# Taking the query projection from a transposed copy of x, with the layer norm folded into the weights and the rotation tables

## What is computed

```
xn   = layernorm(x)                       # per row: (x - mean) * (var + 1e-5)^-0.5
q    = rope(xn @ Wq);  k = rope(ctx @ Wk);  v = ctx @ Wv      # 32 heads of 16; ctx has 256 features
x1   = x + tanh(g_x) * (softmax(q k^T / 4) v @ Wout + bout)
r    = layernorm(x1)
y    = relu(r @ up)^2 @ down + (r @ expert) * (sum of the top 2 of r @ gate)
out  = x1 + tanh(g_f) * (layernorm(y) * gamma + beta)
```

## Time and profile before

| | |
|---|---|
| median of three runs | 1609.11 us |
| the profiled execution, its own time | 1609.51 us |
| its span in the trace | 1607.7 us (1.8 us lie around it) |
| PE busy | 1552.5 us, 97% |
| DVE busy | 976.1 us, 61% |
| ACT busy | 638.1 us, 40% |
| POOL busy | 296.2 us, 18% |
| DMA queue of the kernel | 27.8% of the 16 engines' span |

### The profile page before, as it was taken

How to read it: one execution, slowest core, us unless ns; L and a number is a source line. 1 busy time by engine, 2 the same in 40 slices (tenths; PEclk the granted TensorE clock), 3 DMA queues, 4 the chain that set the end, 5 groups by cost and what they waited for, 6 DMA issues and landing times.

```text
span 1607.7 us, 26049 instructions
## 1 busy us (share of the span) xinstructions
PE 1552.5 (97%) x9818; PEld 1158.5 (72%) x9818; DVE 976.1 (61%) x1448; ACT 638.1 (40%) x962; POOL 296.2 (18%) x370
## 2 busy tenths in 40 slices
PE   8799999999999999988999999999999999999997
PEld 6466666666666666654887887878878878788786
DVE  7887777887887777765663535426444354353524
ACT  4365555555555555556442222222222222222221
POOL 5222222222222222201010102002010020010202
PEclk9799999999999999999999999999999999999999
DMA  6644443444444344333530101101000011010101
GB/s 173 142 114 109 108 102 104 126 104 124 127 124 116 97 107 102 96 89 117 154 105 1 53 27 33 47 2 53 27 27 33 21 47 33 14 46 21 53 0 40
DMA packets 67192, 121.24 MB, mean 75 GB/s; under 512 B 12280, under 2 KB 25720, under 8 KB 67064
## 3 DMA queue, kind: packets, MB, share of 16 engines
q1 hardware_dynamic: 67064, 119.50, 27.8%
HBM read 51.17 MB, written 16.78 MB: 42 GB/s over the span
## 4 chain that ended last, share of the span: by engine, by line
PE 84%; DVE 11%; issue 2%; ACT 1%; POOL 1%; DMA 0%; POOLq 0%; DVEq 0%; ACTq 0%; SPq 0%
PE pP L986 16%; PE pA L1183 11%; PE pO L986 11%; PE pB L1183 11%; PE pT L986 10%; PE pO L1108 6%; PE pA L1080 6%; DVE mneg L1402 5%; PE pM L986 4%; PE pB L1096 2%; PE pT L993 2%; PE pP L993 2%; PE pM L993 2%; PE pM L1150 1%; DVE rot L1330 1%
## 5 line engine op out<-in xcount | busy, mean ns | idle before, releaser
L1402 DVE TENSOR_REDUCE mneg<-pA 128x4 f32<-128x1024 f32 x250 | 305.6, 1223 | 137.1 <-PE pA L1080 135.3
L887 ACT ACTIVATE probs<-pB 128x1024 f32<-128x1024 f32 x249 | 255.2, 1025 | 259.5 <-PE pB L1096 249.4
L1505 DVE TENSOR_TENSOR relu<-relu 128x512 f32<-128x512 f32 x128 | 89.0, 695 | 257.4 <-ACT hid L939 257.4
L704 POOL TENSOR_SCALAR var_eps<-meanvar 128x1 f32<-128x1 f32 x96 | 34.5, 360 | 1048.4 <-DVE meanvar L1287 1048.2
L1183 PE MATMUL pA<-dn,hid 128*128 128x512 f32 x768 | 198.6, 394 | 0.7
L1183 PE MATMUL pB<-dn,hid 128*128 128x512 f32 x768 | 196.0, 390 | 0.0
L986 PE MATMUL pP<-fT,up 128*128 128x512 f32 x768 | 190.3, 396 | 0.0
L986 PE MATMUL pO<-fT,up 128*128 128x512 f32 x768 | 187.6, 393 | 0.0
L1183 PEld LDWEIGHTS pA<-dn,hid 128*128 128x128 f32 x768 | 143.2, 188 | 35.7 <-DVE hid L1507 4.2
L986 PEld LDWEIGHTS pO<-fT,up 128*128 128x128 f32 x768 | 144.3, 188 | 32.6 <-issue 0.7
L1183 PEld LDWEIGHTS pB<-dn,hid 128*128 128x128 f32 x768 | 144.2, 188 | 31.0
(11 more groups left out here) (199 smaller groups left out, 1971.3 us busy)
## 6 DMA issues: line engine op xcount, KB each, us to landing
stk<-kT SPq DMA_DIRECT2D x180, 128.0 KB, 2.9
stq<-qT SPq DMA_DIRECT2D x180, 128.0 KB, 3.0
fres<-x_scratch SPq DMA_DIRECT2D x34, 256.0 KB, 2.8
xin<-x SPq DMA_DIRECT2D x32, 256.0 KB, 3.0
xres<-x SPq DMA_DIRECT2D x32, 256.0 KB, 3.3
x_scratch<-xres SPq DMA_DIRECT2D x32, 256.0 KB, 2.3
out<-y_s SPq DMA_DIRECT2D x32, 256.0 KB, 2.0
fx<-x_scratch SPq DMA_DIRECT2D x29, 256.0 KB, 2.7
```

The costliest lines, as they stand in the source:

```text
L704: nc.gpsimd.tensor_scalar_add(var_eps[:], meanvar[:, 1:2], EPS).then_inc(ve_made, 1)
L887: nc.scalar.activation(probs[:, s % 4, :, :, :].rearrange("p a b s -> p a (b s)"), psum[:, :, :], ACT.Exp).then_inc(exp_done, 1)
L1402: nc.vector.tensor_reduce(mneg[par][:, :, 2 * u:2 * u + 2].rearrange("p t q -> p q t"), psum[:, :, :].rearrange("p q (t k) -> p q t k", t= ...
L1505: nc.vector.tensor_tensor(r[:], r[:], r[:], ALU.mult).then_inc(sq_made, 1)
```

## The change

The query projection no longer starts from a normalised x that TensorE turns. The host gives a second copy of x, already turned, `xT`, with 128 features of each of four chunks on the partitions. With the weights Wq centred once (from each column its mean over the 512 features is subtracted), `x @ Wc` equals `(x - mean(x)) @ Wq`, so the mean of each row falls out. The row's `rstd` is a factor of each output row, and it is multiplied into this row tile's entries of the cosine and sine tables, after K has used them and before Q does.

What this does to the engines, for batches 2 to 15 (0 and 1 keep the old way in the opening):

- TensorE: X0 and X1 go (8 transposes an iteration). ScalarE: their two rounding copies go. VectorE: their two subtractions go, and the two `ln_apply`. The statistics stay.
- SP: `load_xT` twice an iteration, 256 KB each, into the tile `xn`; half 1 ahead of `load_x(i+3, 0)` and so of the residual, half 0 ahead of `load_x(i+3, 1)`. It waits until the half before has been split. `load_x` now waits for the statistics instead of `xn`.
- GpSimd: `split_x` twice an iteration (a rounding copy and a subtraction, 128x512 each): half 1 between `rope_sum` Q0 and `rope_sum` K1, half 0 after `rope_sum` Q1. TensorE's Q job waits for it (`xT_split`).
- VectorE: before each Q it scales two pieces of 128x32, of `cos_t` and of `sin_t`, and waits for both before the rotation.
- Once, at the end of the opening: 8 matmuls for the column means into pO, a copy of them by ScalarE (which takes part of its list ahead of the tanh of the gates), four transfers of Wq again, and on GpSimd 12 instructions of 128x512 (`centre_weights`). The first exponential and the fourth wait for 2 and 4 of the 4 chunks, since the raw weights lie in `probs`; Q0 of batch 2 waits for all.
- SBUF: `rden`, `aT`, `gt_s` and `gt_raw` move, two temporary tiles lie under `aT`, and there are two `rstd`.

```diff
@@ -65,12 +65,12 @@
...
-    0: ("X0", "a10"),
+    0: ("a10",),
...
-    5: ("X1", "kT0"),
+    5: ("kT0",),
@@ -217,6 +218,11 @@
...
             return first.enter_context(nc.sbuf_tensor(name, shape, dt))
+        def under(name, shape, dt=F32):
+            with nc.sbuf_tensor(name, shape, dt) as tile:
+                return tile
@@ -246,14 +252,19 @@
...
         attn = [sb1(f"attn{t}", [P, D]) for t in range(TT)]
-        rden = [sb1(f"rden{i}", [P, NH // 2]) for i in range(2)]
-        aT = [sb1(f"aT{i}", [P, KC, P], F32R) for i in range(2)]
+        aT = []
+        mean_w = under("mean_w", [P, P], F32R)
+        aT.append(sb1("aT0", [P, KC, P], F32R))
+        col_mean = under("col_mean", [P, D])
+        aT.append(sb1("aT1", [P, KC, P], F32R))
         xres = [sb1(f"xres{i}", [P, D]) for i in range(2)]
         gbout = sb1("gbout", [P, D])
+        rden = [sb1(f"rden{i}", [P, NH // 2]) for i in range(2)]
         mneg = [sb1(f"mneg{i}", [P, TT, NH]) for i in range(2)]
...
         rot2.append(sb1("rot21", [P, D]))
+        col_mean = col_mean[:, :]
         rot = {"Q0": rot_q0, "Q1": rot_q1, "K0": rot_k, "K1": rot_k}
@@ -261,6 +272,11 @@
...
         rot_k1 = raw1[0]
+        raw_again = [raw1[k] for k in (0, 1, 6, 7)]
+        def split_no(b, t):
+            return TT * (b - 2) + t + 1
@@ -493,9 +517,17 @@
...
                 if some(n - 1):
-                    sp.wait_ge(xn_made, n - 1)
+                    sp.wait_ge(xn_made if n <= TT * 2 + 1 else st_made, n - 1)
                 alone(sp)
                 sp.dma_start(xin[t][:], xt_d[n]).then_inc(x_in[t], INC)
+            def load_xT(b, t):
+                if (b, t) == (2, 0):
+                    sp.wait_ge(*done_of("X1", 1))
+                else:
+                    sp.wait_ge(xT_split, 2 * (split_no(b, t) - 1))
+                alone(sp)
+                sp.dma_start(xn[:], xT[b * TT + t]).then_inc(xT_in, INC)
@@ -549,6 +581,8 @@
...
+                if within(b2):
+                    load_xT(b2, 1)
@@ -558,6 +592,7 @@
...
+                    load_xT(i + 3, 0)
@@ -690,25 +730,49 @@
...
             last.then_inc(consts_made, 1)
+            nc.gpsimd.memset(mean_w[:].bitcast(F32), 1.0 / D).then_inc(mean_w_made, 1)
...
-            def inv_std(count):
+            def inv_std(count, t=0):
                 pool.wait_ge(mv_made, count)
...
                 pool.wait_ge(ve_made, count)
-                nc.gpsimd.tensor_tensor(rstd[:], var_eps[:], neg_half[:], ALU.pow).then_inc(rstd_made, 1)
+                nc.gpsimd.tensor_tensor(rstds[t][:], var_eps[:], neg_half[:], ALU.pow).then_inc(rstd_made, 1)
...
                 nc.gpsimd.tensor_tensor(t1, t1, rot2[ROPES.index(name) % 2][:], ALU.add).then_inc(roped, 1)
+            def split_x(b, t):
+                n = split_no(b, t)
+                used, of = ("Q0", b) if t else ("Q1", b - 1)
+                pool.wait_ge(*done_of(used, of))
+                pool.wait_ge(xT_in, INC * n)
+                alone(pool)
+                xv = xn[:].rearrange("p (c s) -> p c s", c=KC)
+                nc.gpsimd.tensor_copy(xnT[0][:], xv).then_inc(xT_split, 1)
+                pool.wait_ge(xT_split, 2 * n - 1)
+                nc.gpsimd.tensor_tensor(xnT[1][:], xv, xnT[0][:].bitcast(F32), ALU.subtract).then_inc(xT_split, 1)
+            def centre_weights():
+                pool.wait_ge(col_made, 1)
+                for c in range(KC):
+                    pool.wait_ge(w_again[c], INC)
+                    nc.gpsimd.tensor_tensor(raw_again[c], raw_again[c], col_mean, ALU.subtract).then_inc(centred, 1)
+                    pool.wait_ge(centred, 3 * c + 1)
+                    nc.gpsimd.tensor_copy(wq_s[0][:, c, :], raw_again[c]).then_inc(centred, 1)
+                    pool.wait_ge(centred, 3 * c + 2)
+                    nc.gpsimd.tensor_tensor(wq_s[1][:, c, :], raw_again[c], wq_s[0][:, c, :].bitcast(F32),
+                                            ALU.subtract).then_inc(centred, 1)
@@ -736,9 +800,17 @@
...
+                        if name == "Q0":
+                            split_x(b2, 1)
...
+                    if i < 0:
+                        split_ctx(i + 3, (par + 1) % 2)
+                    split_x(i + 3, 0)
+                    if i < 0:
+                        centre_weights()
...
-                    split_ctx(i + 3, (par + 1) % 2)
+                    if i >= 0:
+                        split_ctx(i + 3, (par + 1) % 2)
@@ -877,6 +949,8 @@
...
                             act.wait_ge(w_lo, W1 - CC - 2)
+                        if i == 0 and s in (0, 3):
+                            act.wait_ge(centred, 3 * 2 if s == 0 else 3 * KC)
                         if isinstance(i, int) and i == 0 and s in (1, 2):
@@ -919,6 +993,8 @@
...
                     job(value, -1, -1)
+            act.wait_ge(col_done, 1)
+            nc.scalar.copy(col_mean, pO[:, :]).then_inc(col_made, 1)
             later_setup()
@@ -1030,6 +1106,12 @@
...
                         job(value, -1, -1)
+                pe.wait_ge(mean_w_made, 1)
+                for c in range(KC):
+                    for w in range(2):
+                        last = nc.tensor.matmul(pO[:, :], mean_w[:], wq_s[w][:, c, :],
+                                                start=(c == 0 and w == 0), stop=(c == KC - 1 and w == 1))
+                last.then_inc(col_done, 1)
                 pe.wait_ge(o_taken, len(OPENING))
@@ -1038,6 +1120,10 @@
...
                 elif name[0] == "Q":
+                    if not opened(name, b):
+                        if (b, t) == (2, 0) and half != 1:
+                            pe.wait_ge(centred, 3 * KC)
+                        pe.wait_ge(xT_split, 2 * split_no(b, t))
                     last = product(psum, lambda a, c: xnT[a][:, c, :], lambda w, c: wq_s[w][:, c, :], KC, half)
@@ -1324,6 +1410,14 @@
...
+                    if name[0] == "Q" and not opened(name, b):
+                        dve.wait_ge(rstd_made, n + 1)
+                        dve.wait_ge(*taken_of(f"K{t}", b))
+                        alone(dve)
+                        for side in (cos_t, sin_t):
+                            own = side[:, n, :, :, :].rearrange("p w k l -> p (w k l)")
+                            nc.vector.tensor_scalar(own, own, rstds[t][:, 0:1], None, ALU.mult).then_inc(scaled, 1)
+                        dve.wait_ge(scaled, 2 * split_no(b, t))
                     nc.vector.tensor_tensor(view(rot_of(name, b)), xv, table(cos_t), ALU.mult)
@@ -1420,12 +1514,8 @@
...
                         ln_statistics(i + 2, 1)
-                    elif s == 3 and within(i + 2) and not first:
-                        ln_apply(i + 2, 1)
                     elif s == 14 and within(i + 3):
                         ln_statistics(i + 3, 0)
-                    elif s == 15 and within(i + 3):
-                        ln_apply(i + 3, 0)
@@ -1566,6 +1656,7 @@
...
+        "xT": a["x"].reshape(NT, P, KC, P).transpose(0, 3, 2, 1).reshape(NT, P, D),
```

32 lines of the change are left out of this document (23 added, 9 removed), and 4 rows, old and new, of tables (BANK, LAG).

## The result

The changed kernel takes **1615.62 us** (median of 5 runs, 1614.77 to 1619.30), the kernel before 1609.11 in the same session (5 runs, 1608.59 to 1610.73): a ratio of **1.0045, 95% interval 1.0032 to 1.0059**. The forecast was 1615.0. The total was right by luck and its composition wrong: phase 1 became more than twice as much slower as forecast, and phase 2, priced at nothing, became faster by most of the difference. The profiled execution took 1615.62 us with a span of 1613.8.

A forecast was written before the change was run, and what follows sets the result against it. It took TensorE's list and the logits-reduction loop through VectorE as pacing by turns. -0.03 + 0.21 + 0.10, about +0.3 an iteration, gave 3.7; with opening 2.0 and crowded transfers 0.2, 5.9 us: 1615.0, range 1604.5 to 1624.

The forecast's parts named there:

- Steps 0 to 6: -0.03 an iteration: TensorE saves 1.3 us, but VectorE's scaling of 0.42 before Q0 leaves 0.03 gained; bounds -0.20 to +0.15 us.
- Steps 7 and 8: +0.21: Q1 waits for GpSimd's split, late because the residual lands 0.62 later: +0.21 us an iteration, bounds -0.12 and +0.8.
- Step 9: +0.10: Q1's scaling costs VectorE 0.42, idle time covers 0.32, so 0.10 us an iteration stays; bounds 0 and 0.28.
- Rival 4: TensorE's 1.3 us stand at step 5 lowers the clock, 1.5 us an iteration: 20 us, 1635; chance 0.04.
- Rival 3: VectorE's scalings beside GpSimd's additions or K1 sum lose up to 1 us twice an iteration: 1625 to 1640; chance 0.06.
- Iteration 0: 0: Iteration 0 has no residual, so no late split; its scalings cost what its freed transposes give: 0.
- The end of the opening: +2.0: Column-mean matmuls and copy delay the tanh table, gates, `gbout` and first reduction: +2.0 us, bounds +1.7 and +5.
- Phase 2 is the same instructions. The new places in SBUF are priced at nothing: Phase 2 was to stay unchanged, since the new SBUF places change no instruction's shape: 0 us.

The follow-up runs named there:

- the variants: Changed kernel with early GpSimd split and six filler transposes at step 5: 1604.04 us (scaling 0.65); changed kernel with scaling moved to steps 3 and 8: 1612.73 us (1.27).
- the runs with tanh first: Changed kernel with ScalarE's two tanh activations ahead of the column means' copy: 1615.84 us; with three other edits too, 1596.08, against 1594.83 without this one.
- GpSimd's split first: Changed kernel with GpSimd's split of half 1 ahead of the two residual additions instead of behind Q0's rotation sum: 1616.78 us.

## Why the prediction was right in total and wrong in its parts

- **"Steps 0 to 6: -0.03 an iteration"**: right. Step 4 came 0.45 us earlier, the scaling cost 0.39 (0.42 forecast), step 6 moved by -0.04. And the scaling was indeed what ate the gain: moved away, with the split early, it gives back 44.90 - 44.33 = 0.57 an iteration.
- **"Steps 7 and 8: +0.21"**: the mechanism was right, the size and the spread were not. The term took one landing of `xres` for all, 13.7 us into the iteration, and moved it by the 0.62 of issue alone. The transfer itself became slower behind xT (median from issue to landing 3.3 before, 3.8 after, on the pages), so it lands some 1.1 us later, and it had never been regular: the additions start 12.6 to 14.8 us into the iteration before and 13.7 to 15.6 after. Q1 waited 0 to 1.4 us; the seven iterations that waited cost 5.6 us, 0.43 an iteration where 0.21 was forecast. The upper bound (+0.8 for a residual 1.2 us later) had it.
- **"Step 9: +0.10"**: not seen. The undisturbed iteration is 44.88 to 44.91, -0.07 against before, where the sum without the split was to be +0.07. In the one that begins at 293.51 the scaling pair starts at 321.15 and the reduction at 322.77, 29.26 us into the iteration; before it was 29.29. All of the iteration ahead of it had come a little earlier, and that covered the 0.10.
- **Rival 4, the clock, "chance 0.04"**: this happened, in four of 13 steady iterations and once in iteration 0. Its price (1.5 us each) was right; that it would be every iteration or none was the mistake, and so was its reason against (around that wait TensorE is busy without a break). It cost 6.1 us.
- **Rival 3, the scaling meets GpSimd, "chance 0.06"**: it didn't happen in the changed kernel, where no scaling takes over 0.24 us. The mechanism is real, as the 0.65 and 1.27 us of the variants show; the prediction was right that GpSimd's list has nothing at these places.
- **"Iteration 0: 0"**: it cost 2.08. The granted clock rose later (0.50 from 68 to 72 us, 0.98 before) and fell again behind a wait of 1.74 us at 82.11.
- **"The end of the opening: +2.0"**: the order of events came as worked out (table load 46.34, `gbout` 47.96, first reduction +2.33). But the runs with tanh first say that the total doesn't depend on it: what starts later here is lost in the variation of iteration 0.
- **"Phase 2 is the same instructions. The new places in SBUF are priced at nothing"**: the step that failed worst, -8.5 us. No row that I chose was from phase 2. The trace of before had it: 395 and 391 ns for one product in alternating blocks is not noise in work that is identical but for a tile's place.

Forecast: 3.7 + 2.0 + 0.2 = 5.9. Measured in phase 1 up to the last iterations: 2.33 + 2.08 + 10.58 = 15.0, less 9 behind it. Two errors of 9 us each cancelled, and neither had anything to do with the other. That the range held the time is luck: with the gate weights in their old place the same prediction would have met 1624.3, just outside it.

## What to carry to other kernels

Where a change moves tiles, compare the mean of one matmul between stretches that differ only in which buffer they use, before the change as well; for fp32 products like these, keep the operands of a pair at equal places modulo 512 B. Time taken from an engine that another one paces becomes a stand, and a stand of TensorE can have a price of its own in some iterations (1.5 us for one of 1.32 here, nothing for one of 0.90): fill it or shorten it. Two causes that mask each other have to be removed together (+1.2 and -1.9 us apart, -11.6 together), so a step that gives nothing alone isn't thereby useless. Count the events behind a time (falls, late starts) in more than one trace: here two kernels with the same phase 1 had them in different iterations.

## What the runs showed of the hardware

- A 128x128 by 128x512 fp32 matmul with its weight load repeats every 226.6 to 228.4 ns with both tiles at the same place modulo 512 B, and every 231.9 to 234.5 at a distance of 32, 96, 128, 192, 224, 384, 448 or 480 B; over phase 2 with all pairs off, 105.04 us a block against 102.78.
- The granted clock fell behind a stand of 1.32 us in 4 or 5 of 13 iterations (in 7 with GpSimd's split first) and not in the others with the same stand; it fell behind none of 0.90. Behind Q1's waits it fell after 1.99, 2.07, 2.40 and 2.50 us, and not after 2.33 nor after any up to 1.56.
- A VectorE scaling of 128x32 in SBUF takes 0.22 us and repeats after 0.14. Beside GpSimd's rounding copy of 128x512 it took up to 0.65 us, and beside its sum of 128x512 up to 1.27.
